# Spreading FP4 scales by TensorE, and a reordered last head in three cross-attention layers

## The chip, the cores and the metric

The kernel runs on one core of a Trainium2 chip, in one launch. The metric is the device time of that launch in microseconds (us). The engines are PE (TensorE), DVE (VectorE), ACT (ScalarE), POOL (GpSimd) and SP (SyncE, which here only issues DMAs).

## The reference, cut to what matters

The program is a stack of twelve layers on `x` (2 batches, 128 tokens, 256 features). The change touches three 16-head cross-attention layers (L0, L2, L3) and the four-bit feed-forward layer (L1_ffn).

```python
# L0_xattn, L2_xattn, L3_xattn: 16 heads of 128, context of 2048 tokens
scores = einsum('bhtd,bhsd->bhts', q, k) / scale      # masked
attn = softmax(scores)                                # P
out = einsum('bhts,bhsd->bhtd', attn, v) @ Wo
x = x + out
...
# L1_ffn: gate, up and down weights are 4-bit codes times scales
W = fp4_value(code) * scale                           # one scale per 32 inputs (two codes a byte)
h = gelu_tanh(x @ Wgate.T) * (x @ Wup.T)              # 256 -> 2048
x = x + h @ Wdown.T
```

For the four-bit layer the scales of gate and up are 8 rows of 2048 numbers each: row `a` holds the scales for the 16 partitions 16a to 16a+15 of a weight tile (8 rows for 128 partitions). Down has 8 rows of 2048 too, so a scale table has 8 x 6144 numbers.

## The kernel before, in words

Each layer is one block; all engines leave a block together (PE, ACT, DVE, POOL and SP meet at its end), and the block of a layer also issues, on SP, the loads of the next layer's weights into the other of two arenas. A block starts with a layer norm on DVE and ACT, and PE turns the result (`xn` to `xnT`).

**Four-bit layer, `fp4_layer` (line 1392).** The codes (3 MB) and the scales are loaded during the block before. The scales are written to all 128 partitions by eight broadcasting DMAs of 16 partitions each (line 214), 384 KB each, 3 MB together, behind the codes in the same queue. The weights are made in eight parts: parts 0 to 3 are quarters of gate and up (512 columns of codes each), parts 4 and 5 the second halves of gate and up (1024), parts 6 and 7 halves of down (1024). For each part DVE masks the bytes (`bytes_of`, line 1476), ACT multiplies by 4097 (`spread`, line 1457), and DVE shifts and masks twice, ORs (`weights`, lines 1492 to 1494) and then multiplies by the scales in two passes (line 1500), which ends with `w_ready` counted up. Before part 0's product with the scales DVE waits for all loads of the arena, `wait_weights` (the last statement before line 1500). PE waits for `w_ready` 2 before the first four column groups `q` of gate and up (line 1436), for 4 before the next four, and for 6 before the last eight; then it multiplies with down (line 1444). DVE forms `inter` from ACT's gelu and PE's up product (line 1508) in `products`: it stands between the parts, as `weights` 0 to 4, products 0 to 3, `weights(5)`, products 4 to 7, `weights(6)`, and so on. All of this is DVE program order.

**16-head layers, `xattn_layer` (line 291).** A unit is one head of one batch, 32 units in all: unit 8i+u is head u//2 of group i, batch u%2. ACT and DVE form P of a unit as two float16 parts, high (ACT line 599) and low (DVE line 729), each in two halves. SP turns both by DMA transpose (lines 377 and 384), and PE multiplies them with the context values: `mix_high` (line 474, 32 matmuls) and `mix_low` (line 484, 16 matmuls), into bank `O[h]`. Per head, ACT copies `O` to `oT` (line 603), PE multiplies by the value weights (`tail_values`, 518), ACT copies (`values_copy`, 609) and PE adds the head's output into bank `OUT` (`tail_out`, 523). The last unit is not turned by DMA: PE turns it (`turn_last`, line 496, part 0 high and part 1 low, 16 transposes each), ACT and DVE copy it back (633, 791) and `mix_last` (509) multiplies it. `scores` fills PE up to three units ahead, so that in the last three units PE has no scores to do. In L2 and L3 POOL also prepares experts' weights for a later layer (lines 2994 to 3011), in the same block.

## Time and profile before

| | us |
|---|---|
| median of 3 runs (lowest, highest) | 1417.43 (1414.89, 1417.97) |
| the profiled execution, its own time | 1408.27 |
| its span, first to last instruction | 1406.5 |
| PE, DVE, ACT, POOL busy | 1231.5, 1088.9, 916.2, 304.7 |

The table reads as follows: the profiled execution lies below the three timed runs, so durations taken from it are set against its own time. The span is what the trace covers; 1.8 us lie around it. Busy PE time includes work that only keeps the engine active (`keep_busy`, line 180).

### The profile page before, as it was taken

Reading aid. Unit: us, or ns where it says so; the run is one execution under the profiler, and the core shown is the slowest. Engines: PE = TensorE matmul, PEld = TensorE weight load, DVE = VectorE, ACT = ScalarE, POOL = GpSimd, SP = SyncE. Lnnn points to the kernel's source line nnn. Section 1 sums busy time; section 2 is a strip of 40 time slices with the busy share of each in tenths; the row PEclk is TensorE's granted clock in tenths of the full one; section 3 lists DMA queues with packets and bytes.
Section 4 is the critical chain, followed back from the end, with each engine's and each line's share of the span. In section 5 each row is a group of like instructions: output and inputs, shape, how many; then the busy total and the mean of one; then the engine's idle time right before and its main releaser. Section 6 shows DMA issues by size and latency. Waiting matters only on the chain. (4 is left out here: it accounts for less than half of the span.)

```text
span 1406.5 us, 25870 instructions
## 1 busy us (share of the span) xinstructions
PE 1231.5 (88%) x10035; PEld 846.6 (60%) x10035; DVE 1088.9 (77%) x2028; ACT 916.2 (65%) x1283; POOL 304.7 (22%) x235
## 2 busy tenths in 40 slices
PE   7999998478879888876989999978898899999987
PEld 3677776353335555555756766765685567666654
DVE  6877885686888999837488898955796798899564
ACT  5877775635667877732267777745695767677664
POOL 3000000001241110000006164250362063452400
PEclk9999999889999999988999999999999999999999
DMA  7999997001008999984169998950662889889700
GB/s 281 178 189 184 179 180 137 18 27 71 1 13 155 193 197 192 200 170 118 55 115 196 175 198 172 174 144 0 208 201 90 149 165 176 171 168 169 141 8 8
DMA packets 548587, 195.77 MB, mean 139 GB/s; under 512 B 534913, under 2 KB 535297, under 8 KB 546945
## 3 DMA queue, kind: packets, MB, share of 16 engines
q1 hardware_dynamic: 548480, 194.35, 69.0%
q8 instruction: 67, 1.10, 0.3%
q14 instruction: 40, 0.32, 0.1%
HBM read 59.83 MB, written 0.26 MB: 43 GB/s over the span
## 5 line engine op out<-in xcount | busy, mean ns | idle before, releaser
L729 DVE SCALAR_TENSOR_TENSOR arena<-L_xattn_sm,L_xattn_rr,arena 128x1024 f16<-128x1024 f32 x192 | 279.0, 1494 | 9.4 <-ACT arena L599 9.4
L460 PE MATMUL ps<-ctxT,L_xattn_qk 128*128 128x512 f16 x1152 | 265.5, 380 | 0.8 <-DVE L_xattn_mx L711 0.5
L584 ACT ACTIVATE L_xattn_sm<-L_xattn_sm,L_xattn_mx 128x2048 f32<-128x2048 f32 x96 | 192.2, 2002 | 78.9 <-DVE L_xattn_mx L711 78.1
L599 ACT ACTIVATE arena<-L_xattn_sm,L_xattn_rr 128x1024 f16<-128x1024 f32 x192 | 210.1, 1141 | 5.2
L474 PE MATMUL ps<-arena,ctx 128*128 128x128 f16 x2976 | 186.0, 222 | 18.4 <-DMA arena<-arena 18.3
L474 PEld LDWEIGHTS ps<-arena,ctx 128*128 128x128 f16 x2976 | 174.5, 99 | 33.1 <-DMA arena<-arena 22.6
L460 PEld LDWEIGHTS ps<-ctxT,L_xattn_qk 128*128 128x128 f16 x1152 | 111.1, 98 | 126.3 <-issue 3.2
L711 DVE CUSTOM_DVE_ANT_0 L_xattn_sm<-ps,L_xattn_bias 128x1024 f32<-128x1024 f32 x96 | 117.2, 1221 | 65.7 <-issue 65.4
L711 DVE CUSTOM_DVE_ANT_0 L_xattn_sm<-ps,L_xattn_bias,L_xattn_mx 128x1024 f32<-128x1024 f32 x96 | 123.2, 1284 | 1.0 <-issue 0.4
L484 PEld LDWEIGHTS ps<-arena,ctx 128*128 128x128 f16 x1488 | 90.8, 98 | 17.1
L484 PE MATMUL ps<-arena,ctx 128*128 128x128 f16 x1488 | 98.3, 219 | 0.0
L180 PE MATMUL ps<-ctxT,identh 128*128 128x512 f16 x328 | 86.9, 401 | 7.6 <-PEq L361 3.0
L2277 PE MATMUL ps<-arena 128*128 128x512 f16 x384 | 92.1, 391 | 0.0
L2289 PE MATMUL ps<-L_xattn_pt,arena 128*32 128x128 f16 x1024 | 70.4, 226 | 22.8 <-DMA L_xattn_pt<-L_xattn_pp 22.4
L2289 PEld LDWEIGHTS ps<-L_xattn_pt,arena 128*32 128x32 f16 x1024 | 59.9, 100 | 41.7 <-DMA L_xattn_pt<-L_xattn_pp 32.2
L589 ACT ACTIVATE L_xattn_rr<-L_xattn_raw,L_xattn_anyone 128x1 f32<-128x1 f32 x96 | 28.2, 293 | 85.8 <-DVE L_xattn_raw L721 84.9
L2419 ACT ACTIVATE L_xattn_pp<-L_xattn_sm,L_xattn_rr 128x1024 f16<-128x1024 f32 x64 | 70.0, 1140 | 20.8 <-DVE L_xattn_rr L2610 20.8
L2619 DVE SCALAR_TENSOR_TENSOR L_xattn_pp<-L_xattn_sm,L_xattn_rr,L_xattn_pp 128x1024 f16<-128x1024 f32 x64 | 79.6, 1285 | 2.7 <-ACT L_xattn_pp L2419 2.4
L2592 DVE CUSTOM_DVE_ANT_0 L_xattn_sm<-ps,arena 128x1024 f32<-128x1024 f32 x64 | 76.5, 1222 | 4.0 <-issue 3.7
L2407 ACT ACTIVATE L_xattn_sm<-L_xattn_sm,L_xattn_nm 128x2048 f32<-128x2048 f32 x32 | 64.1, 2002 | 19.1 <-DVE L_xattn_nm L2601 19.1
L2994 POOL TENSOR_TENSOR L_xattn_inv<-bits,L_xattn_exp 128x48 int32<-128x48 int32 x8 | 2.1, 264 | 304.9 <-DVE L_xattn_exp L2964 304.9
L2277 PEld LDWEIGHTS ps<-arena 128*128 128x128 f16 x384 | 36.2, 100 | 43.8 <-issue 5.1
(541 smaller groups left out, 2107.0 us busy)
## 6 DMA issues: line engine op xcount, KB each, us to landing
L_ffn_ring<-in_L_ffn_experts SPq DMA_DIRECT2D x34, 384.0 KB, 3.8
arena<-in_L_xattn_w SPq DMA_DIRECT2D x36, 320.0 KB, 4.0
arena<-in_L_ffn_experts SPq DMA_DIRECT2D x8, 768.0 KB, 8.7
arena<-in_L_xattn_w SPq DMA_DIRECT2D x6, 640.0 KB, 10.3
arena<-arena SPq DMA_TRANSPOSE x193, 4.5
arena<-in_L_ffn_codes SPq DMA_DIRECT2D x1, 3072.0 KB, 11.4
arena<-in_L_ffn_scales SPq DMA_DIRECT2D x8, 384.0 KB, 22.9
arena<-in_L_attn_w SPq DMA_DIRECT2D x1, 2163.0 KB, 19.2
```

Source lines behind the costliest of these rows:

```text
L180: k.nc.tensor.matmul(k.ps[:, bank, :], k.identh[:], k.ctxT[:, 0, 0, 0:512] if data is None else data, start=True, stop=True)
L460: last = nc.tensor.matmul(ps[:, at, :], qk[:, h // 2, qp, h % 2, b * P:(b + 1) * P], k.ctxT[:, cp, b, at * 512:(at + 1) * 512], start=(a = ...
L474: last = nc.tensor.matmul(O[h][:, b * P:(b + 1) * P], k.ctx[:, cp, b * KT + kt, :], pt[:, b, 0, kt, :], start=(kt == 0 and cp == 0), stop= ...
L484: last = nc.tensor.matmul(O[h][:, b * P:(b + 1) * P], k.ctx[:, 0, b * KT + kt, :], pt[:, b, 1, kt, :], start=False, stop=(kt == KT - 1), s ...
L584: nc.scalar.activation(sm[:, u % 2, :], sm[:, u % 2, :], ACT.Exp, bias=mx[:, u % 2, 1:2], scale=-1.0, accum_out=rs[:, u % 2:u % 2 + 1]).th ...
L599: nc.scalar.mul(pp[:, u % 2, 0, at], sm[:, u % 2, at], rr[:, u % 2:u % 2 + 1]).then_inc(s.p_high, 1)
L711: nc.vector.tensor_tensor_reduce(sm[:, u % 2, half * 1024:(half + 1) * 1024], ps[:, 2 * half:2 * half + 2, :].rearrange("p a n -> p (a n)" ...
L729: nc.vector.scalar_tensor_tensor(pp[:, u % 2, 1, at], sm[:, u % 2, at], rr[:, u % 2:u % 2 + 1], pp[:, u % 2, 0, at], ALU.mult, ALU.subtrac ...
L2277: last = nc.tensor.matmul(ps[:, at, :], qm[:, h % 4, qp, b * P:(b + 1) * P], knT[:, kp, h // 8, b, at * 512:(at + 1) * 512], start=(a == 0 ...
L2289: last = nc.tensor.matmul(O[h // 4][j:j + 32, b * P:(b + 1) * P], v[:, b * KT + kt, h, :, :].rearrange("p s d -> p (s d)"), pt[:, b, part, ...
L2592: nc.vector.tensor_tensor_reduce(sm[:, u % 2, half * 1024:(half + 1) * 1024], ps[:, 2 * half:2 * half + 2, :].rearrange("p a n -> p (a n)" ...
L2619: nc.vector.scalar_tensor_tensor(pp[:, u % 2, 1, at], sm[:, u % 2, at], rr[:, u % 2:u % 2 + 1], pp[:, u % 2, 0, at], ALU.mult, ALU.subtract)\
```

## The change

It does two things.

1. **Four-bit layer.** The scale table is laid out anew, so that the scales of parts 0 to 3 are its first 2048 columns. These are loaded once, as 8 rows (64 KB, semaphore `scale_rows`), and the eight broadcasting DMAs carry only the other 4096 columns. POOL builds an 8x128 selection matrix `sel`, and PE multiplies it with those rows: four float32 matmuls of 512 columns, into PSUM banks 3, 4, 7 and 0. DVE reads the scales of parts 0 to 3 from there. `bytes_of` of parts 4 to 7 moves behind `weights(1)`, and `wait_weights` now stands before part 4's product. `keep_busy` goes from 14 to 16 matmuls and stands behind the four.

2. **16-head layers.** In the last iteration, `turn_last(0)` moves ahead of `mix_high` of unit 30, `turn_last(1)` ahead of its `mix_low`, and `mix_last(0)` ahead of `tail_out` of head 14. Batch 1 of the last head accumulates in bank `PREP` in place of its half of `O[1]`, so the last head's two batches leave one by one (`values_last`, `out_last`, on ACT `mixed_last`, `values_copy_last`).

```diff
-            for a in range(8):
-                sp.dma_start(dst[16 * a:16 * a + 16, :], src[a].partition_broadcast(16)).then_inc(sem, 16)
+            sp.dma_start(dst[0:8, 0:MLP], src[:, 0:MLP]).then_inc(k.g.scale_rows, 16)
+            for a in range(8):
+                sp.dma_start(dst[16 * a:16 * a + 16, MLP:], src[a, MLP:].partition_broadcast(16)).then_inc(sem, 16)
...
+                nc.gpsimd.affine_select(out=sel[:], in_=k.ones[0:8, :], ...).then_inc(s.sel_part, 1)
+                pool.wait_ge(s.sel_part, 1)
+                nc.gpsimd.affine_select(out=sel[:], in_=sel[:], ...).then_inc(s.sel_ready, 1)
...
-                keep_busy(k, 7, 14)
-                pe.wait_ge(g.xnT_ready, k.xt + 1)
+                pe.wait_ge(g.scale_rows, 16)
+                pe.wait_ge(s.sel_ready, 1)
+                for i in range(4):
+                    if i == 3:
+                        pe.wait_ge(g.xnT_ready, k.xt + 1)
+                    nc.tensor.matmul(ps[:, SPREAD[i], :], sel[:], scales[0:8, scale_at[i]:scale_at[i] + FIRST],
+                                     start=True, stop=True).then_inc(s.sc_ready, 1)
+                keep_busy(k, 1, 16)
...
-                for i in range(2, len(parts)):
-                    bytes_of(i)
+                bytes_of(2)
+                bytes_of(3)
...
-                    if i == 0:
+                    if i < 4:
+                        dve.wait_ge(s.sc_ready, i + 1)
+                        scale = ps[:, SPREAD[i], :]
+                    else:
                         wait_weights(k, dve, slot, loaded)
...
-                for i in range(5):
+                weights(0)
+                weights(1)
+                for i in range(4, len(parts)):
+                    bytes_of(i)
+                for i in range(2, 5):
                     weights(i)
```

```diff
+                def values_last(b):
+                    pe.wait_ge(s.oT_ready, XH + b)
+                    at = slice(b * P, (b + 1) * P)
+                    nc.tensor.matmul(TAIL[1 - b][:, at], wv[1], oT[:, at], start=True, stop=True).then_inc(s.oh_psum, 1)
+                def out_last(b):
+                    pe.wait_ge(s.oh_ready, XH + b)
+                    nc.tensor.matmul(OUT[:, b * D:(b + 1) * D], oh[:, b * P:(b + 1) * P], wo[1][:, 1, :], start=False,
+                                     stop=True, skip_group_check=True).then_inc(s.out_done, 1)
...
                         if final and u == UNITS - 1:
+                            mix_last(0)
                             tail_out(*mixed)
                             break
+                        if final and u == UNITS - 2:
+                            turn_last(0)
                         mix_high(i, u, first)
...
                         if final and u == UNITS - 2:
-                            turn_last(0)
+                            turn_last(1)
                         mix_low(i, u)
...
-                turn_last(1)
-                mix_last(0)
-                mix_last(1)
-                tail_values(LASTI, BODY - 1, False)
-                tail_out(LASTI, BODY - 1)
+                values_last(0)
+                mix_last(1)
+                out_last(0)
+                values_last(1)
+                out_last(1)
```

PE at the end of a 16-head layer, before, from `mix_low` of unit 29 on (L474 and L484 are `mix_high` and `mix_low`, L496 `turn_last`, L509 `mix_last`):

```order
L484 MATMUL ps<-arena,ctx 128x128 x16
L474 MATMUL ps<-arena,ctx 128x128 x32
L518 MATMUL ps<-L_xattn_oT,arena 128x256
L496 MATMUL ps<-identh,arena 128x128 x16
L484 MATMUL ps<-arena,ctx 128x128 x16
L523 MATMUL ps<-arena,L_xattn_oh 128x256 x2
L496 MATMUL ps<-identh,arena 128x128 x16
L509 MATMUL ps<-arena,ctx 128x128 x48
L518 MATMUL ps<-L_xattn_oT,arena 128x256
L523 MATMUL ps<-arena,L_xattn_oh 128x256 x2
```

The same stretch of PE in the changed kernel (L531 is `values_last`, L535 `out_last`):

```order
L484 MATMUL ps<-arena,ctx 128x128 x16
L496 MATMUL ps<-identh,arena 128x128 x16
L474 MATMUL ps<-arena,ctx 128x128 x32
L518 MATMUL ps<-L_xattn_oT,arena 128x256
L496 MATMUL ps<-identh,arena 128x128 x16
L484 MATMUL ps<-arena,ctx 128x128 x16
L509 MATMUL ps<-arena,ctx 128x128 x32
L523 MATMUL ps<-arena,L_xattn_oh 128x256 x2
L531 MATMUL ps<-L_xattn_oT,arena 128x128
L509 MATMUL ps<-arena,ctx 128x128 x16
L535 MATMUL ps<-arena,L_xattn_oh 128x256
L531 MATMUL ps<-L_xattn_oT,arena 128x128
L535 MATMUL ps<-arena,L_xattn_oh 128x256
```

Both groups of transposes have moved ahead of a group of unit 30, 32 of the 48 matmuls of L509 have moved ahead of a pair of L523, and the closing pair of steps is cut into two batches.

DVE in the four-bit layer, before, from the layer norm's last row on (L1476 is `bytes_of`):

```order
L139 TENSOR_SCALAR xn<-x,mv,rstd 128x256 x2
L1476 TENSOR_SCALAR arena<-arena 128x512 x2
L1476 TENSOR_SCALAR arena<-arena 128x1024 x4
L1492 TENSOR_SCALAR L_ffn_m<-arena 128x512
L1493 TENSOR_SCALAR arena<-arena 128x512
L1494 TENSOR_TENSOR L_ffn_m<-L_ffn_m,arena 128x512
L1500 TENSOR_TENSOR L_ffn_wgu<-L_ffn_m,arena 128x512 x2
```

The same stretch of DVE in the changed kernel (L1522 is `bytes_of`, L1550 the product with the scales):

```order
L139 TENSOR_SCALAR xn<-x,mv,rstd 128x256 x2
L1522 TENSOR_SCALAR arena<-arena 128x512 x2
L1538 TENSOR_SCALAR L_ffn_m<-arena 128x512
L1539 TENSOR_SCALAR arena<-arena 128x512
L1540 TENSOR_TENSOR L_ffn_m<-L_ffn_m,arena 128x512
L1550 TENSOR_TENSOR L_ffn_wgu<-L_ffn_m,ps 128x512 x2
L1538 TENSOR_SCALAR L_ffn_m<-arena 128x512
L1539 TENSOR_SCALAR arena<-arena 128x512
L1540 TENSOR_TENSOR L_ffn_m<-L_ffn_m,arena 128x512
L1550 TENSOR_TENSOR L_ffn_wgu<-L_ffn_m,ps 128x512 x2
L1522 TENSOR_SCALAR arena<-arena 128x1024 x4
```

The four long `bytes_of` have moved behind two parts, and the product of the first parts reads `ps` in place of `arena`.

PE at the start of the four-bit layer in the changed kernel, between the turning of `xn` and the first column group; before, the row of L1470 was not there and that of L180 had 14 matmuls:

```order
L190 MATMUL ps<-ident,xn 128x128 x4
L1470 MATMUL ps<-arena,L_ffn_sel 128x512 x4
L180 MATMUL ps<-ctxT,identh 128x512 x16
L1482 MATMUL ps<-xnT,L_ffn_wgu 128x256 x64
```

The four spreading matmuls stand ahead of the work that only keeps PE active.

## Rows read from the trace of the kernel before

**Rows 1.** The waits: engine, tile and line, releaser: us, times, longest.

```profile
DVE L_ffn_wgu L1500 <- DMA arena<-in_L_ffn_scales: 7.6, 1, 7.6
DVE x L794 <- PE ps L523: 15.6, 3, 5.2
```

**Rows 2.** Timeline of the four-bit layer: start, us, engine, line [idle before <-releaser].

```profile
629.80 3.17 DVE L1476 TENSOR_SCALAR arena<-arena 128x512 int32<-128x512 int32 x6
...
630.87 5.76 PE L180 MATMUL ps<-ctxT,identh 128*128 128x512 f16 x14
...
632.88 0.42 DVE L1492 TENSOR_SCALAR L_ffn_m<-arena 128x512 int32<-128x512 int32 x1
...
641.93 1.30 DVE L1500 TENSOR_TENSOR L_ffn_wgu<-L_ffn_m,arena 128x512 f32<-128x512 f16 x2 [7.57 <-DMA arena<-in_L_ffn_scales]
...
646.11 0.43 DVE L1492 TENSOR_SCALAR L_ffn_m<-arena 128x512 int32<-128x512 int32 x1
...
646.23 15.78 PE L1436 MATMUL ps<-xnT,L_ffn_wgu 128*128 128x256 f32 x64 [9.59 <-DVE L_ffn_wgu L1500]
...
663.13 14.09 PE L1436 MATMUL ps<-xnT,L_ffn_wgu 128*128 128x256 f32 x64 [1.12 <-DVE L_ffn_wgu L1500]
...
691.07 0.76 DVE L1523 SCALAR_TENSOR_TENSOR x<-ps,x 128x256 f32<-128x256 f32 x2 [12.88 <-PE ps L1444]
```

**Rows 3.** Busy time by windows: PE, PEld, DVE, ACT, POOL, then granted clock, DMA.

```profile
636.00:638.00 2.00, 0.63 (x3) 0.13 (x1) 0.00 (x0) 1.81 (x2) 0.00 (x0) 0.98 1.13 156
```

**Rows 4.** Lines 1476, 1375 and 3386: durations ns min/median/max, starts, forms.

```profile
L1476 DVE TENSOR_SCALAR arena<-arena x8: 421/559/691, 626.7 to 632.3; 128x512 int32<-128x512 int32 x4, 128x1024 int32<-128x1024 int32 x4
L1375 DVE TENSOR_TENSOR x<-ps,x x1: 692/692/692, 625.5 to 625.5; 128x512 f32<-128x512 f32 x1
L3386 POOL TENSOR_SCALAR_AFFINE_SELECT upper<-ones x1: 293/293/293, 3.5 to 3.5; 128x128 f32<-128x128 f32 x1
```

**Rows 5.** The eight scale loads, issued from 607.5 to 610.8: issue to landing.

```profile
DMA to landing us min/median/max: 14.2/22.9/31.0
```

**Rows 6.** Timeline of the end of L0_xattn.

```profile
225.22 2.19 ACT L599 ACTIVATE arena<-L_xattn_sm,L_xattn_rr 128x1024 f16<-128x1024 f32 x2
...
228.09 1.96 PE L474 MATMUL ps<-arena,ctx 128*128 128x128 f16 x32 [2.22 <-DMA arena<-arena]
...
233.08 1.06 PE L496 MATMUL ps<-identh,arena 128*128 128x128 f16 x16
...
233.97 2.84 PE L509 MATMUL ps<-arena,ctx 128*128 128x128 f16 x48
...
237.29 0.70 PE L518 MATMUL ps<-L_xattn_oT,arena 128*128 128x256 f32 x2 [0.47 <-ACT L_xattn_oT L603]
...
238.45 1.13 PE L523 MATMUL ps<-arena,L_xattn_oh 128*128 128x256 f32 x4 [0.46 <-ACT L_xattn_oh L609]
...
239.62 0.69 DVE L794 TENSOR_TENSOR x<-ps,x 128x512 f32<-128x512 f32 x1 [5.20 <-PE ps L523]
...
240.82 1.28 ACT L147 ACT_TABLE_LOAD   x1 [2.42 <-PEq L361]
```

**Rows 7.** Timeline of the end of L2_xattn.

```profile
920.27 2.19 ACT L599 ACTIVATE arena<-L_xattn_sm,L_xattn_rr 128x1024 f16<-128x1024 f32 x2
...
921.08 1.96 PE L474 MATMUL ps<-arena,ctx 128*128 128x128 f16 x32 [1.17 <-DMA arena<-arena]
...
930.90 2.92 POOL L3011 TENSOR_TENSOR arena<-arena,L_xattn_exp 128x768 bf16<-128x768 f32 x2
...
932.63 0.69 DVE L794 TENSOR_TENSOR x<-ps,x 128x512 f32<-128x512 f32 x1 [5.20 <-PE ps L523]
...
934.25 1.28 ACT L147 ACT_TABLE_LOAD   x1 [2.84 <-PEq L361]
```

**Rows 8.** Timeline of the end of L3_xattn.

```profile
1313.98 2.91 POOL L3011 TENSOR_TENSOR arena<-arena,L_xattn_exp 128x768 bf16<-128x768 f32 x2
...
1316.21 0.69 DVE L794 TENSOR_TENSOR x<-ps,x 128x512 f32<-128x512 f32 x1 [5.20 <-PE ps L523]
```

More of the change, by code:

```diff
@@ L508, in mix_last @@
                             for cp in range(2 - part):
-                                last = nc.tensor.matmul(O[1][:, P:2 * P], k.ctx[:, cp, KT + kt, :], pt[:, 1, part, kt, :],
+                                last = nc.tensor.matmul(PREP[:, P:2 * P], k.ctx[:, cp, KT + kt, :], pt[:, 1, part, kt, :],
                                                         start=(kt == 0 and cp == 0 and part == 0),
@@ L626, in body @@
                             q_copy(*group)
+                        if final and u == UNITS - 2:
+                            last_copy(0, 0)
+                            last_copy(0, 1)
                         if head:
                             values_copy(*head, first and u == 2)
-                def last_copy(part, half):
-                    act.wait_ge(s.last_psum, 2 * part + half + 1)
-                    act.wait_ge((s.mixed_hi, s.mixed_lo)[part], XH * B - 2)
-                    nc.scalar.copy(pt[:, 1, part, half * KT // 2:(half + 1) * KT // 2, :], TURNED[2 * part + half])\
-                        .then_inc((s.last_hi, s.last_lo1)[part], 1)
-                if opening:
-                    act.wait_ge(g.keys_loaded1, 16)
-                    nc.scalar.copy(k.ctxT[:, 0, 1, :], raw_context(k, 1)[0]).then_inc(g.keys_high1, 1)
                 q_copy(0, 0)
@@ L656, in _ @@
                 iterations(act, body)
[L657 to L658 removed]
                 last_copy(1, 1)
[L660 to L661 removed]
+                mixed_last(0)
+                values_copy_last(0)
+                mixed_last(1)
+                values_copy_last(1)
             @block.gpsimd
@@ L1409, in fp4_layer @@
         gelu = sb("gelu", [P, RING, T])
+        sel = sb("sel", [8, P])
         inter = k.arena[slot][:, 3 * MLP:5 * MLP].rearrange("p (q t) -> p q t", q=NG)
@@ L1419, in _ @@
                 stage_loads(sp)
+            @block.gpsimd
+            def _(pool):
+                nc.gpsimd.affine_select(out=sel[:], in_=k.ones[0:8, :], compare_op=ALU.is_ge, fill=0.0, base=0,
+                                        pattern=[[1, P]], channel_multiplier=-16).then_inc(s.sel_part, 1)
+                pool.wait_ge(s.sel_part, 1)
+                nc.gpsimd.affine_select(out=sel[:], in_=sel[:], compare_op=ALU.is_ge, fill=0.0, base=15,
+                                        pattern=[[-1, P]], channel_multiplier=16).then_inc(s.sel_ready, 1)
             @block.tensor
@@ L1495, in weights @@
                     vals = mm.bitcast(F16).rearrange("p (n a) -> p n a", a=2)
-                    if i == 0:
+                    if i < 4:
+                        dve.wait_ge(s.sc_ready, i + 1)
+                        scale = ps[:, SPREAD[i], :]
+                    else:
                         wait_weights(k, dve, slot, loaded)
+                        scale = scales[:, scale_at[i]:scale_at[i] + width]
                     to = at % MLP
@@ L1500, in weights @@
                         last = nc.vector.tensor_tensor(dests[at // MLP][:, par, to:to + width], vals[:, :, par],
-                                                       scales[:, at:at + width], ALU.mult)
+                                                       scale, ALU.mult)
                     last.then_inc(s.w_ready, 1)
@@ L3487, in lay_out @@
                                         rows(L("L1_ffn_down_W_packed").T)], axis=1)
-    d["L1_ffn_scales"] = np.concatenate([L("L1_ffn_gate_scales").T, L("L1_ffn_up_scales").T,
+    halves = [L(f"L1_ffn_{w}_scales").T[:, h * MLP // 2:(h + 1) * MLP // 2] for h in range(2) for w in ("gate", "up")]
+    d["L1_ffn_scales"] = np.concatenate([*halves,
                                          L("L1_ffn_down_scales").T.reshape(8, 8, D).transpose(1, 0, 2).reshape(8, -1)],
```

29 lines of the change are left out of this document (22 added, 7 removed).

## The prediction

> **What bounds the kernel now.** I read the waits first, then the timelines of the two places that the change touches. No single engine bounds the whole program: each layer has its own chain, and a layer's start follows from the end of the one before. So what matters is which wait ends last inside the two kinds of block.
>
> In the four-bit layer one wait stands out: DVE stands still for 7.6 us before its first product with the scales, and the releaser is the load of the scales [rows 1]. The reader is to see in the timeline that it is a true stop: DVE has part 0 unpacked at 641.93 - 7.57 = 634.36, and PE, behind it, starts its first column group only at 646.23, after 9.6 us idle [rows 2]. The last of the eight scale loads was issued at 610.8 and they take up to 31.0 us to land, which ends at 641.8 [rows 5]; that is the release. After it DVE is busy without a gap until 663.1, and PE, which has done its first eight column groups by 662.0 (646.23 + 15.78), waits 1.12 us for DVE's parts 4 and 5 [rows 2]. From 663.13 on PE runs through gate, up and down to DVE's last step at 691.07, 27.9 us later [rows 2]. So the layer's end hangs on when DVE finishes part 5, and that on when it may begin to multiply by the scales.
>
> At the end of the 16-head layers the last wait is DVE's for the last `tail_out`: 15.6 us in three layers, 5.2 each [rows 1]. In L0 it sets the block's end: DVE ends at 240.31 and the next block's first row on ACT is at 240.82, 0.51 later [rows 6]. In L2 it does not: DVE ends at 933.32, but the next block's row comes at 934.25, 0.93 later; POOL's last row ends at 933.82, 0.43 ahead of it [rows 7]. In L3 both end together, POOL at 1316.89 and DVE at 1316.90 [rows 8].
>
> **Four-bit layer.** DVE first. Before, six `bytes_of` stand between the layer norm and part 0, from 629.80 to 632.88 [rows 2]. A short one is 0.42 us and a long one 0.69 [rows 4]; overlapped they fill 3.08 us, some 0.7 for the two short and 2.4 for the four long. Only the short ones stay ahead, so part 0's unpacking starts at 630.5. It takes 634.36 - 632.88 = 1.48 and is done at 632.0.
>
> Then DVE waits for the first spreading matmul. PE could start it where it now starts `keep_busy`, at 630.87 [rows 2]. Its rows are loaded ahead of all broadcasts; the first broadcast, six times as large, took 14.2 us from 607.5 [rows 5], so the rows are there by 622. `sel` takes POOL two operations of 0.29 each [rows 4] at the block's start, while PE is idle until 630, so by 628. A float32 matmul of 256 columns is two records, 14.09 / 64 = 0.22 us apart at the high clock [rows 2], so one of 512 columns is 0.88, and 1.76 at the low one. The clock is low at 631: fourteen float16 matmuls of 512 columns take 5.76 us, 0.41 each, which is 1.2 GHz [rows 2], and it is high (0.98 granted, 2.4 GHz) only between 636 and 638, after PE had been active since about 630 [rows 3]. So the first spread ends at 630.87 + 1.7 plus 0.2 to drain, 632.8, and DVE loses 0.85 us to it. If the spreads were free of this, that 0.85 would be gained too (upper bound); the later ones, at 634.5, 636.2 and 637.1, are ahead of DVE.
>
> DVE needs 646.11 - 641.93 = 4.18 us from the first product to the end of part 1's [rows 2]: 632.85 + 4.18 = 637.03. The four long `bytes_of` now stand here, in the way: 2.4, so 639.45. From part 2's first row to the release of part 5 it was 663.13 - 646.11 = 17.02; that gives 656.45, against 663.13: 6.7 us earlier. Behind the moved `bytes_of` ACT's multiplications of parts 4 to 7 come later, but part 4 is wanted only 5.7 us later.
>
> The product now reads its scales from PSUM. A DVE operation with 512 columns and one operand in PSUM took 0.69 [rows 4], two from SBUF take 1.30 [rows 2], 0.65 each; eight of them cost at most 0.3, and I take 0.1. **Sum for this layer: 6.6 us.**
>
> The Trainium skill speaks against this step here: "VectorE: DVE Perf Modes", section "The TRN2 errata — SBUF-src ops pay a fixed extra latency per instruction", gives a Vector operation with a PSUM source 120 fixed cycles and one with SBUF sources 58. By it the eight products would cost 0.5 us more, the layer would gain 6.2, and the time would be 1409.7; the rows above bear out less.
>
> PE must not become the bound. After the spreads (637.1) come sixteen `keep_busy` of 0.22 at the high clock, until 640.6; eight column groups take 14.1 (64 records, as in the second half [rows 2]), until 654.7, 1.8 us ahead of DVE. The remaining scales, two thirds of the bytes, are wanted by part 4's product at about 647.7, while all landed at 641.8 before [rows 5]. So these edits lie under DVE's work; the two extra `keep_busy` and SP's ninth DMA too. If the clock rose only with the column groups, PE would be 2.3 us late (a rival below).
>
> **L0.** `turn_last(0)` is put into PE's wait for the DMA transpose: PE idles 2.22 us up to 228.09. It waits for the last P-high, whose second half is ready at 225.22 + 2.19 = 227.41. Sixteen transposes take 233.97 - 233.08 = 0.89, the second eight 0.45: done at 227.9, so `mix_high` of unit 30, which is queued behind, still starts at 228.09 [rows 6]. What follows holds 0.89 us less and one half-width value matmul more (some 0.25): the last mixing ends at 236.81 - 0.64 = 236.17. ACT's copies of the turned P-high come at 228 to 230, before it is wanted elsewhere. From that end to DVE's add it was 239.62 - 236.81 = 2.81, two PE steps of 0.70 and 1.13 and two copies of ACT among it [rows 6]. With one batch left, PE's steps shrink by about 0.25 and 0.48 and the copies by 0.1 each (a half-width operation keeps its fixed part), and `out_last(0)` stands in the way by 0.1: 1.97. DVE would start at 238.14, **1.5 us earlier**. Bounds: 0.6 if the halves cost as much as wholes, 2.0 if everything halves.
>
> **L2 and L3.** Here the wait that is filled is shorter, 1.17 us in L2: `mix_high` starts at 921.08, but P-high is complete only at 920.27 + 2.19 = 922.46. With the second eight transposes `mix_high` starts at 922.95, 1.87 later [rows 7]. Less 0.89, plus 0.25, less 0.84 at the tail: DVE ends 0.4 us later, at 933.7. With 0.51 behind it that is 934.2, just what POOL sets now (934.25): nothing lost, nothing gained. That cover gone, it would cost 0.4. In L3 POOL ends with DVE, so at most 0.1 can be had [rows 8], and at worst L2's 0.4 is lost. I take zero for both.
>
> **Sum:** 6.6 + 1.5 + 0 + 0 = 8.1 us. The profiled execution's own time is 1408.27 (span 1406.5), so it would be 1400.2. The median of the runs is 9.2 higher, and there the same difference gives **1409.3**.
>
> **Rivals.**
> *All three 16-head layers gain 1.5.* For it: the same 5.2 us wait in each [rows 1]. Against: POOL's ends [rows 7, 8] and the late P-high. It takes 3.0 more: 1406.3.
> *PE bounds the four-bit layer.* If the spreads and `keep_busy` all run at the low clock, they end at 630.9 + 4 x 1.71 + 16 x 0.43 = 644.6, the column groups at 658.7 instead of 656.4: 2.3 us of the gain go, 1411.6. For it: the clock was low for 6 us after PE began [rows 2, 3]; against: PE now stays active without a break.
> *The four-bit layer gives back nearly all*, because something in part 4's way (its scales, ACT's multiplications) takes the place of the wait: only L0's 1.5 stays, 1415.9. Against: 5.9 us between the old landing and the new need.
> *Slower: the scale rows land late.* PE's spreads, and all of PE behind them, wait for one small DMA. If its eight long rows landed only with the end of the queue, at 641.8, the first product would follow at 643.7, PE (idle meanwhile, clock low) would do the other spreads by 648.8 and the sixteen matmuls by about 653.5, and eight column groups by 667.6. That is 4.5 later than 663.1; with L0's 1.5, 1420.4. It decides from a landing at about 637 on that nothing is gained in this layer. Against: it is issued first, and a larger load behind it took 14.2 us [rows 5].
>
> **How the numbers follow.** Chances: forecast 0.62, all three layers 0.13, PE bound 0.16, gain given back 0.06, late rows 0.03. A measurement of this kernel can tell about 0.2%, 2.8 us, from no change. The first three are faster by more: 0.91; given back is within it: 0.06; late rows: 0.03 slower. The forecast's own bounds (0.85 up in the four-bit layer and 0.5 in L0; 0.9 in L0, 0.2 for PSUM and 0.8 in L2 and L3 down) span 1407.9 to 1411.2. With the two neighbouring cases, 1406.3 and 1411.6, and the scatter of 3 us among the runs before, the range is 1405.4 to 1413.2.
>
> **What would show it.** Right: DVE's first product with the scales near 633 to 634, waiting for PE under 1 us; PE's first column group near 640.5; DVE still the releaser before the ninth group, some 6.5 us earlier counted from the block's start; in L0 the add 1.5 us earlier from the last P-high; in L2 the same distance to the next block, with a gap before L474. Wrong: a DVE wait for PE of several us, L1436's successor starting at the low clock, or POOL ending well before the blocks of L2 and L3.

## The result, and the profile after

| us | before | after |
|---|---|---|
| median (lowest to highest, runs) | 1417.43 (1414.89 to 1419.47, 5) | 1406.71 (1402.35 to 1409.59, 5) |
| profiled execution, its own time | 1408.27 | 1406.71 |
| its span | 1406.5 | 1405.0 |
| mean granted TensorE clock in it | 0.964 | 0.962 |

The ratio on record is 0.9912, with a 95% interval of 0.9895 to 0.9929: 12.5 us less, 10.0 to 14.9. The forecast was 8.1 less. The direction was right. The size was too small: 0.9912 of 1417.43 is 1405.0, just under the range's lower end of 1405.4. The five runs of each kernel in the table give a smaller difference than that ratio: 10.7 us between the medians, and 10.7 between the means (1417.3 and 1406.6). By them the changed kernel's 1406.71 lies inside the range, near its lower end; the record does not show what makes the two figures differ. And the two profiled executions are only 1.5 us apart, so what the profiles show and what the runs show has to be told apart. One run of the experiments below, the sixth of f2, took 2109.57 us at a mean granted clock of 0.553 and is left out of every figure.

The four-bit layer in the timeline of the changed kernel (start, us, engine, line, and in brackets the idle time before it and its releaser). They answer to [rows 2]:

```profile
629.20 1.28 ACT L147 ACT_TABLE_LOAD   x1 [3.34 <-PEq L1301]
629.56 0.36 POOL L1458 TENSOR_SCALAR_AFFINE_SELECT L_ffn_sel<-L_ffn_sel 8x128 f32<-8x128 f32 x1
632.71 1.13 PE L190 MATMUL ps<-ident,xn 128*128 128x128 f32 x4 [4.80 <-DVE xn L139]
633.24 0.42 DVE L1538 TENSOR_SCALAR L_ffn_m<-arena 128x512 int32<-128x512 int32 x1
633.77 7.19 PE L1470 MATMUL ps<-arena,L_ffn_sel 8*128 8x512 f32 x8
635.95 1.28 DVE L1550 TENSOR_TENSOR L_ffn_wgu<-L_ffn_m,ps 128x512 f32<-128x512 f16 x2 [1.23 <-PE ps L1470]
640.89 5.53 PE L180 MATMUL ps<-ctxT,identh 128*128 128x512 f16 x16
646.26 15.92 PE L1482 MATMUL ps<-xnT,L_ffn_wgu 128*128 128x256 f32 x73
657.09 2.36 DVE L1550 TENSOR_TENSOR L_ffn_wgu<-L_ffn_m,arena 128x1024 f32<-128x1024 f16 x2
```

The reader is to see that the stop of 7.57 us is gone: DVE waits 1.23 us for the first spread and is busy from there on. PE's column groups have no idle time in their row. Its sixteen groups begin at 646.26 and the product with down at 673.88, so the first eight end half way, at about 660.1, while DVE released part 5 at 657.09 + 2.36 = 659.45. So PE, not DVE, is now last, by 0.6 us.

The same stretch by windows (PE, PEld, DVE, ACT, POOL busy; then granted clock, DMA share, GB/s):

```profile
633.77:640.90 7.13, 7.13 (x10) 2.50 (x9) 5.73 (x11) 1.70 (x4) 0.00 (x0) 0.50 0.91 247
640.90:644.30 3.40, 3.40 (x10) 1.19 (x10) 3.33 (x7) 3.40 (x4) 0.00 (x0) 0.50 1.03 423
644.30:646.20 1.90, 1.90 (x9) 0.92 (x8) 1.83 (x5) 1.72 (x2) 0.00 (x0) 0.87 0.40 162
646.30:660.30 14.00, 14.00 (x67) 12.72 (x66) 13.72 (x20) 3.34 (x8) 0.00 (x0) 1.00 0.00 0
```

PE was busy for 7.1 us without a break in the first window, and the granted clock stayed at 0.50 (1.2 GHz). It rose at about 644.8 (0.87 over the third window), 3.9 us after the full-row filling matmuls had begun. In the kernel before it rose at about 636.1 (0.98 over the window of [rows 3]), 5.2 us after its filling matmuls had begun [rows 2].

The waits, which answer to [rows 1] (us, times, longest):

```profile
DVE x L821 <- PE ps L535: 19.1, 3, 6.4
DVE L_ffn_wgu L1550 <- PE ps L1470: 1.2, 1, 1.2
```

DVE's wait for the last `tail_out` is longer, 6.4 us for 5.2, though L0's end comes sooner: DVE now stops earlier (its copy of P-low ends sooner), and waits more. The sum of a wait says little about the path.

The ends of L0, L2 and L3, for [rows 6 to 8]:

```profile
229.00 2.19 ACT L612 ACTIVATE arena<-L_xattn_sm,L_xattn_rr 128x1024 f16<-128x1024 f32 x2
230.20 0.62 PE L496 MATMUL ps<-identh,arena 128*128 128x128 f16 x8 [0.56 <-ACT arena L612]
231.24 0.62 PE L496 MATMUL ps<-identh,arena 128*128 128x128 f16 x8 [0.42 <-ACT arena L612]
231.74 1.96 PE L474 MATMUL ps<-arena,ctx 128*128 128x128 f16 x32
...
241.75 0.69 DVE L821 TENSOR_TENSOR x<-ps,x 128x512 f32<-128x512 f32 x1 [6.38 <-PE ps L535]
242.94 1.28 ACT L147 ACT_TABLE_LOAD   x1 [1.98 <-PEq L361]
...
919.74 2.19 ACT L612 ACTIVATE arena<-L_xattn_sm,L_xattn_rr 128x1024 f16<-128x1024 f32 x2
920.94 0.62 PE L496 MATMUL ps<-identh,arena 128*128 128x128 f16 x8 [1.87 <-ACT arena L612]
...
932.43 0.69 DVE L821 TENSOR_TENSOR x<-ps,x 128x512 f32<-128x512 f32 x1 [6.38 <-PE ps L535]
933.62 1.28 ACT L147 ACT_TABLE_LOAD   x1 [1.98 <-PEq L361]
...
1301.59 2.19 ACT L612 ACTIVATE arena<-L_xattn_sm,L_xattn_rr 128x1024 f16<-128x1024 f32 x2
...
1312.22 2.92 POOL L3065 TENSOR_TENSOR arena<-arena,L_xattn_exp 128x768 bf16<-128x768 f32 x2
...
1314.28 0.69 DVE L821 TENSOR_TENSOR x<-ps,x 128x512 f32<-128x512 f32 x1 [6.38 <-PE ps L535]
1315.91 1.28 ACT L174 ACT_TABLE_LOAD   x1 [2.41 <-PEq L361]
```

From the last P-high to the next block's first row: L0 13.94 us where it was 15.60; L2 13.88 for 13.98; L3 14.32 for 14.05. In L0 the add came 12.75 us after the last P-high for 14.40. Of these 1.65 us 0.13 lie ahead of `mix_high` of unit 30 and 1.52 behind its start, where the edit takes work out. In L2 PE now idles 1.87 us before the first eight transposes, waiting for ACT's P-high. In L3 the add came 0.17 us sooner (12.69 for 12.86), but the next block 0.27 later; POOL's last row, not DVE's, ended last there, at 1315.14.

**Where the time went, by layers of the two profiles** (from a layer's first row of the layer norm on DVE, `bn_stats`, to the next layer's):

```
            before   after              before   after
L0_xattn    237.39  239.49   L2_xattn   241.92  244.48
L0_attn      71.68   71.69   L2_attn     52.94   51.94
L0_ffn       26.73   26.71   L2_ffn      85.86   85.59
L1_xattn    267.73  268.17   L3_xattn   244.36  244.76
L1_attn      20.38   20.59   L3_attn     33.42   33.41
L1_ffn       65.00   59.04   L3_ffn      55.64   55.65
```

The four-bit layer is 5.96 us shorter by this count. But its layer norm now begins 0.93 us after the block's start where it was 0.72, and L1_attn, which is counted up to there, grew by those 0.21 (its two short `bytes_of` take 0.97 us for 0.76; what slows them is not shown). From block start to block start it is 5.75 us. So the places that the change touches sum to 5.75 + 1.66 + 0.10 - 0.27 = **7.24 us**. Yet L0_xattn and L2_xattn are longer as wholes, at units that the change doesn't touch. L2's unit 26 shows how. These are the same instructions on PE, before and after:

```profile
879.15 1.13 PE L447 MATMUL ps<-L_xattn_qT,arena 128*128 128x512 f32 x2 [2.19 <-ACT L_xattn_qT L574]
880.11 1.95 PE L474 MATMUL ps<-arena,ctx 128*128 128x128 f16 x32
```

```profile
876.27 1.51 PE L447 MATMUL ps<-L_xattn_qT,arena 128*128 128x512 f32 x2 [2.18 <-ACT L_xattn_qT L587]
877.57 3.25 PE L474 MATMUL ps<-arena,ctx 128*128 128x128 f16 x32
```

```profile
876.30:879.70 3.40, 3.40 (x22) 2.49 (x23) 3.40 (x2) 2.67 (x4) 3.32 (x3) 0.59 0.98 181
883.10:886.50 3.40, 3.40 (x48) 2.81 (x47) 3.27 (x7) 0.68 (x1) 0.00 (x0) 1.00 1.06 196
```

The last two rows are windows of the changed kernel: after PE had idled 2.18 us the granted clock was 0.59 on average for 3.4 us, and the unit took 9.44 us in place of 7.79. In the profile before the same idle time of 2.19 was followed by the high clock. In L0_xattn unit 0 is 1.1 us longer and unit 3 is 3.1 longer (8.13 for 5.00), and both lie over low stretches twice as long as before or not there before; with unit 13's 0.9, for which I found no such stretch, and less the 1.2 by which units 2 and 5 are shorter, they make up for the 1.7 gained at the layer's end and more. In L2_xattn another 0.7 lies ahead of unit 30 (6.09 for 5.38 between its exponential and the one before). With plain copies in place of the DMA transposes that interval is 5.32 or 5.33 in each kernel of the first series below, so it hangs on the transposes; whether the change has a part in it is open.

### The profile page after: what moved, and what is told of

The parts are those of the page before. It is cut to its first block and busy times, and to the rows that moved or that the text cites. A ratio compares the mean times of both kernels' runs of the same rounds, so it can differ in the third digit from the quotient of the medians.

```text
span 1405.0 us, 25920 instructions
## 1 busy us (share of the span) xinstructions
PE 1237.8 (88%) x10051; PEld 848.8 (60%) x10051; DVE 1088.2 (77%) x2028; ACT 916.3 (65%) x1289; POOL 305.4 (22%) x237
## 5 line engine op out<-in xcount | busy, mean ns | idle before, releaser
L474 PE MATMUL ps<-arena,ctx 128*128 128x128 f16 x2976 | 188.8, 223 | 11.9 <-DMA arena<-arena 11.7
L474 PEld LDWEIGHTS ps<-arena,ctx 128*128 128x128 f16 x2976 | 177.4, 100 | 26.9 <-DMA arena<-arena 15.6
L484 PEld LDWEIGHTS ps<-arena,ctx 128*128 128x128 f16 x1488 | 90.8, 98 | 17.1
L484 PE MATMUL ps<-arena,ctx 128*128 128x128 f16 x1488 | 98.3, 219 | 0.0
L180 PE MATMUL ps<-ctxT,identh 128*128 128x512 f16 x330 | 86.3, 397 | 7.6 <-PEq L361 3.0
L180 PEld LDWEIGHTS ps<-ctxT,identh 128*128 128x128 f16 x330 | 31.6, 101 | 49.6 <-issue 24.3
```

The costliest lines, as they stand in the source:

```text
L180: k.nc.tensor.matmul(k.ps[:, bank, :], k.identh[:], k.ctxT[:, 0, 0, 0:512] if data is None else data, start=True, stop=True)
L474: last = nc.tensor.matmul(O[h][:, b * P:(b + 1) * P], k.ctx[:, cp, b * KT + kt, :], pt[:, b, 0, kt, :], start=(kt == 0 and cp == 0), stop= ...
L484: last = nc.tensor.matmul(O[h][:, b * P:(b + 1) * P], k.ctx[:, 0, b * KT + kt, :], pt[:, b, 1, kt, :], start=False, stop=(kt == KT - 1), s ...
```

## The experiments

The changed kernel was not run again, nor was either edit alone with the DMA transposes in it; only the kernel before was timed again, 40 times beside the experiments. So whether something in the change, with the transposes, brings more than its places show is a rival that stays untested. All kernels that follow hold plain DMA copies of the same bytes in their place, so that P and the last layer's weights are not turned, and their times stand against each other only.

```diff
-sp.dma_start_transpose(pt[:, u % 2, 0, :, :], pp[:, u % 2, 0, :])
+sp.dma_start(pt[:, u % 2, 0, :, :].rearrange("p t q -> p (t q)"), pp[:, u % 2, 0, :])
```

The plain copies land in 2.9 us (median) where the transposes take 4.5. "Tail" below is the time from the last exponential of a 16-head layer to the next block's first row.

### First series: each edit alone

f1 is the kernel before, f2 the changed one, f3 has the four-bit edit alone, f4 that of the 16-head layers alone.

> The kernel before with its 193 + 64 + 8 DMA transposes (P in the cross-attention layers, weights in the last layer) made plain DMA copies of the same bytes, so that P and those weights are not turned: the base for the next three. The time itself may be anything near 1417 us: a copy keeps the order of the work, but its issue and landing may take less than the 2 us and 4.5 us of a transpose. No theory is tested by it alone; its profile shows how much of the 16-head layers' length hangs on the DMA.

> The changed kernel with plain copies. Theory A (each part is worth what its place in the trace shows: four-bit layer 6.0, L0 1.6, L2 0.1, L3 -0.3): 7.4 us under f1. Theory B (part of the gain lies elsewhere, in the cross-attention layers away from the edited places): 10 to 13 us under f1.

> Only the four-bit layer's part of the change, with plain copies. Theory A: 6.0 us under f1. Theory B, if the four-bit part carries the excess: 9 us or more; if not, 6.

> Only the 16-head part, with plain copies. Theory A: 1 to 2 us under f1, nearly all in L0. Theory B: 4 to 7 us under f1, with layers that are shorter ahead of their last three units.

```
                 median us (runs)   L1_ffn   tails L0 / L2 / L3
f1 before        1404.20 (6)        65.00    16.36 / 17.38 / 17.27
f2 both          1405.39 (5)        59.33    16.70 / 18.85 / 19.34
f3 four-bit      1402.24 (4)        59.33    16.37 / 17.27 / 17.38
f4 16-head       1408.68 (6)        64.07    16.70 / 19.33 / 18.90
```

The four-bit edit shortens its layer by 5.7 us (f1 to f3; 5.5 from block start to block start), about as with the real transposes, but the median by 2.0 only. No theory of f2, f3 or f4 came true by the medians: f3 was to be 6 us or more under f1 and is 2.0, f2 was to be 7 us or more under f1 and is 1.2 over it, f4 was to be under f1 and is 4.5 over it. The edit of the 16-head layers *costs* here: 0.34 + 1.95 + 1.63 = 3.9 us at the three tails (f4 less f1), and 4.5 by the medians; f2 less f3 gives 3.9 at the tails and 3.2 by the medians. The reason stands in f2's timeline of L2's end, beside f1's:

```profile
909.41 0.62 PE L496 MATMUL ps<-identh,arena 128*128 128x128 f16 x8 [1.88 <-ACT arena L612]
910.45 1.03 PE L496 MATMUL ps<-identh,arena 128*128 128x128 f16 x8 [0.42 <-ACT arena L612]
911.27 3.15 PE L474 MATMUL ps<-arena,ctx 128*128 128x128 f16 x32
```

```profile
912.19 1.96 PE L474 MATMUL ps<-arena,ctx 128*128 128x128 f16 x32
```

With the turning moved ahead, PE idles 1.88 us for ACT's P-high; then the clock is low (0.61 over 3.4 us) and the 32 matmuls of `mix_high` take 3.15 us for 1.96. With copies that land sooner the wait that was to be filled isn't there, and the moved work makes one. The changed kernel has the same idle times in L2 and L3 (1.87 and 1.40), but in its profiled execution no low stretch fell on them.

### Second series: a pause before each copy

So that PE waits for P as it does for the transposes, SP loads 2 KB and waits for it before each of the 16-head layers' copies.

```diff
+sp.dma_start(little[:], k.ident[:, 0:4]).then_inc(s.pause, 16)
+sp.wait_ge(s.pause, 16 * n)
 sp.dma_start(pt[...].rearrange("p t q -> p (t q)"), pp[...])
```

g1 is the kernel before, g2 both edits, g3 only the moved turning and mixing (no split by batch), g4 only the split (`values_last`, `out_last`, own bank) with the old order. g3 and g4 have the old four-bit layer.

> The kernel before with plain copies in place of the DMA transposes (so P and the last layer's weights are not turned), and in the three 16-head layers a pause ahead of each copy: SP loads 2 KB and waits for it, so that a copy lands some 4.5 to 5 us after its turn begins, as a transpose did. Base for the next three. If the pause does its work, PE's wait before the matmuls of unit 30 in L0 is about 2 us again, and the distance from the last unit's exponential to the next block is 17 to 18.5 us in the three layers.

> The changed kernel with the same stand-in. Read at its places. Theory A (the work moved ahead fills a wait that exists only where the transposed P comes late): from the last exponential to the next block 1.6 us shorter in L0, 0 in L2 and L3, the four-bit layer 6 shorter. Theory C (PE now idles longer in one piece ahead of unit 30, and the clock falls more often in the last stretch): 1.5 us longer in one or both of L2 and L3, with the granted clock at 0.5 in a part of it, as with plain copies.

> Same stand-in; of the 16-head edit only the order (both groups of turning matmuls and the mixing of P-high moved ahead), the last head's two batches still leave together; nothing of the four-bit edit. Theory A: L0 0.7 to 0.9 us shorter than g1, L2 and L3 0.5 to 1.2 us longer where POOL does not hide it. If the order were worth the whole 1.6 in L0, the split would be worth nothing.

> Same stand-in; of the 16-head edit only the split of the last head by batch, with its own bank; order as before; nothing of the four-bit edit. Theory A: 0.8 us shorter than g1 in L0, and in L2 and L3 too unless POOL ends the block (then 0 to 0.4). If the split is worthless: 0 in L0.

```
                 median us (4 runs)     tails L0 / L2 / L3
g1 before        1460.82                22.47 / 19.72 / 20.20
g2 both          1448.58                18.04 / 19.33 / 17.72
g3 order only    1451.48                18.52 / 19.96 / 19.19
g4 split only    1460.48                20.17 / 20.12 / 17.63
```

Here PE does wait, and the whole gains: 12.2 us by the medians (g1 to g2). In the two profiled executions 4.43 + 0.39 + 2.48 = 7.3 stand at the tails and 64.5 - 59.4 = 5.1 in the four-bit layer, 12.4 together; but these two are 19.3 us apart as wholes, so that 12.2 and 12.4 agree is in part luck. Nor are the 7.3 the edit's worth in the changed kernel. The stand-in overshoots: g1's tails are 19.7 to 22.5 us where 17 to 18.5 were expected, its wait ahead of unit 30 in L0 is 3.46 us for about 2, and each of its tails holds a stretch of low clock, g2's only that of L2. The start of `mix_high` of unit 30 in L0, in g1 and in g2:

```profile
247.39 2.71 PE L482 MATMUL ps<-arena,ctx 128*128 128x128 f16 x32 [3.46 <-DMA arena<-arena]
```

```profile
246.62 1.96 PE L482 MATMUL ps<-arena,ctx 128*128 128x128 f16 x32 [0.88 <-DMA arena<-arena]
```

From there to the end of the last `tail_out` it is 13.1 us in g1 and 10.3 in g2, where the kernels with the real transposes have 11.5 and 10.0. So of L0's 4.43 some 1.5 is what the edit gives there, some 1.4 is g1's low stretch, and the rest lies ahead of `mix_high`. Theory A had 1.6 for L0 and nothing for L2 and L3, and its numbers fell in all but L2.

The parts don't come apart so well. By the medians the order alone gives 9.3 and the split alone 0.3; by the tails 4.7 and 4.5. Runs of one kernel lie up to 19 us apart in this series (g2: 1441.4 to 1460.0), so the medians can't tell the one from the other. What the split does is plain in PE's rows of the end of L0, in g4 and g1:

```profile
252.99 1.95 PE L517 MATMUL ps<-arena,ctx 128*128 128x128 f16 x32
254.78 0.44 PE L539 MATMUL ps<-L_xattn_oT,arena 128*128 128x128 f32 x2
...
257.32 0.70 PE L543 MATMUL ps<-arena,L_xattn_oh 128*128 128x256 f32 x2 [0.36 <-ACT L_xattn_oh L649]
```

```profile
254.91 2.84 PE L517 MATMUL ps<-arena,ctx 128*128 128x128 f16 x48
...
259.39 1.13 PE L531 MATMUL ps<-arena,L_xattn_oh 128*128 128x256 f32 x4 [0.46 <-ACT L_xattn_oh L617]
```

From the first of these mixings to the end of the last `tail_out` it is 257.32 + 0.70 - 252.99 = 5.03 us with the split and 5.61 without: 0.6 us. The order takes the sixteen transposes of P-high, 0.9 us [rows 6], out of this tail. The two together are the 1.5 of the forecast, and the 1.52 found behind the start of `mix_high` in the changed kernel.

### Third series: what brings the clock up, and a warm start

h1 is f1 with filling matmuls of 8 rows; h2 is f3 with fourteen more full-row ones in PE's wait at the block's start; h3 and h4 are f3 and f1 again.

```diff
 h1:
-keep_busy(k, 7, 14)
+for _ in range(14):
+    nc.tensor.matmul(ps[:, 7, :], k.identh[0:8, :], k.ctxT[0:8, 0, 0, 0:512], start=True, stop=True)
 h2:
+keep_busy(k, 1, 14)
 xT_tensor(k, pe, k.xn, 0, n, cols=True)
```

> Kernel before with plain copies; the fourteen filling matmuls at the start of the four-bit layer read 8 of their 128 rows (their output is read by nobody). Theory A (matmuls of 8 rows do not bring TensorE's clock up, whatever their data type and whatever they keep the engine busy for): the granted clock stays at 0.5 through the fourteen, each takes the 0.43 us of the low clock, 6.0 us in all, and it is still 0.5 when the first group's matmuls begin 9.6 us later. Rival B (in the change it was the float32 data, or merely that the fall came later, and rows have no part): the fourteen run the last of their row at 0.22 us as they do with 128 rows, and the clock rises during them, 6.8 us after its fall, as in the kernel before.

> Changed four-bit layer alone with plain copies, and fourteen filling matmuls of 128 rows more in TensorE's wait at the layer's start, ahead of the turning of the normed rows (TensorE is idle there for 3.5 us). Theory A: the clock does not fall before the spreads, so they take 3.6 us in place of 7.2; DVE's products of parts 0 to 3 wait less (the first 0.4 to 0.9 us less) and TensorE reaches its first group before DVE has part 1, so that the eighth group ends with DVE's fifth part and not 0.9 us after: the layer becomes 0.9 to 1.7 us shorter than the 59.3 us of the run without it, unless the clock falls during the spreads; then (rival B, 8-row matmuls count as idleness) it falls some 3 us into them, and the gain is 0.9 at most. Rival C: the fillers delay the turning (they last till after the normed rows are there): the layer is the same or up to 1 us longer.

> The changed four-bit layer alone with plain copies, the kernel of the second series again, beside the run above on one chip. If the places of TensorE's low clock fall by chance from one execution to the next, its layer stays at 59.3 us to 0.1, while the sum of the other eleven layers of its profile differs from that of the first time (1343.0) by steps of about 1.6 us, up to some 5 us. If they are fixed by the program, the other eleven are the same to 0.3 us.

> The kernel before with plain copies again, on the same chip as the run above. Its four-bit layer 65.0 us. The difference of the medians to the run above is the four-bit change's worth with plain copies a second time: 5.7 us by the layers of the profiles, and 2.0 by the medians of the second series. Theory A (chance of the low clock's places, with medians of five carrying an error of about 1.5 us each): between 3 and 8 now. Rival B (something in the program takes back 3 to 4 us of the layer's gain each time): 1 to 3 again.

In h1 the clock stayed low through all fourteen, float16 as they are, and on into the column groups. Windows of h1:

```profile
623.20:629.40 6.20, 6.17 (x15) 1.88 (x14) 3.35 (x7) 6.05 (x8) 0.00 (x0) 0.50 1.02 127
639.50:645.00 5.50, 5.46 (x13) 4.41 (x14) 5.33 (x10) 0.47 (x1) 0.00 (x0) 0.50 0.51 208
```

So it is not float32 that kept the clock down in the changed kernel, and not the time for which PE was busy: in the kernel before the clock rose behind the same count of matmuls over 128 rows [rows 2, 3]. The four-bit layer of h1 took 66.1 us; with 128 rows it took 65.0, 64.3 and 66.8 in f1, h4 and i1, so that length tells nothing.

h2's PE in the four-bit layer:

```profile
620.66 3.18 PE L180 MATMUL ps<-ctxT,identh 128*128 128x512 f16 x14 [1.33 <-PEq L1274]
624.13 0.74 PE L190 MATMUL ps<-ident,xn 128*128 128x128 f32 x4 [0.29 <-DVE xn L139]
624.81 3.70 PE L1444 MATMUL ps<-arena,L_ffn_sel 8*128 8x512 f32 x8
628.44 5.31 PE L180 MATMUL ps<-ctxT,identh 128*128 128x512 f16 x16
633.59 14.09 PE L1456 MATMUL ps<-xnT,L_ffn_wgu 128*128 128x256 f32 x64
649.74 15.78 PE L1456 MATMUL ps<-xnT,L_ffn_wgu 128*128 128x256 f32 x64 [2.06 <-DVE L_ffn_wgu L1524]
```

```profile
624.81:628.50 3.69, 3.69 (x10) 1.47 (x10) 3.55 (x8) 1.63 (x3) 0.00 (x0) 1.00 0.88 224
629.50:632.80 3.30, 3.30 (x9) 1.18 (x8) 3.27 (x7) 1.73 (x2) 0.00 (x0) 0.50 1.02 414
650.00:653.30 3.30, 3.30 (x9) 2.56 (x9) 3.27 (x7) 0.00 (x0) 0.00 (x0) 0.50 0.00 0
```

At the high clock (first window) the spreads take 3.70 us in place of 7.19, DVE's wait for the first is gone, and PE is ahead of DVE by 2.06 us before the ninth group, much as the prediction had it (1.8). But about 1 us behind the spreads the clock drops for 3.4 us (second window), and PE's idle 2.06 us is followed by another low stretch (third window), so the last eight groups take 15.78 us for 14.0. The layer is 59.09 us against 59.31: of the 0.9 to 1.7 expected, 0.2. The medians, 1395.81 against 1398.48, differ by less than the runs of either.

h3 and h4 repeat f3 and f1: layers of 59.31 and 64.32 us, medians 1398.48 and 1399.18, 0.7 apart, which is less than either theory of h4 had. Outside the four-bit layer h3's profile is 3.6 us shorter than f3's (1339.4 and 1343.0), the sum of single layers that differ by up to 3.8 us in both directions: L1_xattn took 267.1 and 263.8 us, L3_xattn 242.6 and 246.4, in the same kernel.

### Fourth series: does a layer's length hang on when it starts?

In f1 and h4 L2_xattn took 238.8 and 237.4 us with the old four-bit layer, in f3 and h3 244.0 with the new one (but h1, with the old one, had 244.1, and h2, with the new one, 240.7). That suggested that the edit shifts the later layers against the clock's low stretches, the same way each time. i1 and i3 are f1 and f3 a third time; i2 and i4 have a delay on DVE ahead of the four-bit layer's last add.

```diff
 dve.wait_ge(s.out_psum, 1)
+chain(nc.vector.tensor_tensor(m[:], m[:], m[:], ALU.bitwise_or))              # i2: 1.25 us
+chain(nc.vector.tensor_scalar(m[:, 0:1024], m[:, 0:1024], 0xFF, None, ALU.bitwise_and))  # i4
+chain(nc.vector.tensor_scalar(m[:, 0:512], m[:, 0:512], 0xFF, None, ALU.bitwise_and))    # i4
```

> The kernel before with plain copies, a third time, as the measure for the two kernels with an added pause. Its four-bit layer 64.3 to 65.0 us, its L2_xattn 237.4 to 238.8 us as in both earlier profiles.

> The same, and one operation of 1.25 us more on DVE between the end of the four-bit layer's last product and its add: nothing but 1.3 us of delay for all that follows. Theory A (the other layers' lengths depend on where the stretches of low clock fall against them, and so on how late they start): L2_xattn starts 1.3 us later against the clock's changes, where three kernels of these series had it (the edited four-bit layer's two, and the one with 8-row filling matmuls), and takes 243.9 to 244.1 in place of 238.8 at most; the profile's layers from L2 on are 6.5 us later at L2_attn, and the median of all runs 3 to 7 us above the kernel without the pause. Rival B (layers' lengths have nothing to do with when they start): 1.3 us longer, L2_xattn the same.

> The changed four-bit layer alone, plain copies, a third time. Four-bit layer 59.3 us, L2_xattn 243.9 to 244.0 us as in both earlier profiles; median against the first kernel of this call 0.5 to 3 us less, as twice before, in place of the layer's 5.7.

> The same, and 1.0 us more on DVE at the same place (a row of 1,024 and one of 512 elements). Theory A: L2_xattn then starts where it does in the kernel before, takes 237.4 to 238.8 us, and the kernel with this delay is 3 to 5.5 us faster than the one without; against the first kernel of this call it wins 5 us or more, what the layer itself saved. Rival B: 1.0 us slower than without it.

```
                  median us (runs)   L1_ffn   L2_xattn
i1 before         1402.29 (5)        66.79    242.68
i2 before + 1.25  1403.26 (6)        67.65    239.06
i3 four-bit       1396.13 (6)        59.64    240.27
i4 four-bit +0.96 1394.29 (5)        60.79    242.54
```

Theory A fell. L2_xattn took 242.7 us in the same kernel that had shown 238.8 and 237.4, and 240.3 in the one that had shown 244.0 twice. The delay in i2 cost 1.0 us, about itself; i4 came out 1.8 *faster* than i3 (8.0 under i1), which is inside the scatter of either. So which units meet a low stretch changes from execution to execution of one kernel. The edit's worth in three pairs of medians was 2.0, 0.7 and 6.2; over all 17 and 16 runs the mean spans are 1400.1 and 1397.6, 2.4 us apart, give or take 2.6. The layer's own 5.7 (5.9 on average over the three pairs of profiles, less the 0.2 of its late start) is just outside that. Including the delayed kernels, less their delays, it is 3.7 give or take about 2.2, within which 5.7 lies.

## Why the prediction was off

**Where DVE stands in the four-bit layer: right.** The stop is gone, the products start 6.75 us after the block's start where 6.2 was forecast, DVE waited 1.23 us for the first spread (0.85), because PE came to it 0.34 us later in the block and DVE's product followed its start by 2.18 us for 1.98; DVE itself was ready 0.16 later. "Late scale rows" and "part 4's scales" did not come up: the broadcasting loads landed in 24.1 us at most, against 31.0 before [rows 5], and PE waited for no rows.

**"It is high only between 636 and 638, after PE had been active since about 630", and from that the later spreads at 0.9 us and `keep_busy` at 0.22: this step failed.** It took for granted that the clock would rise behind the spreads, which have 8 rows, as it had behind the filling matmuls of 128 rows. In the changed kernel and in h1 the granted clock stayed at 0.50 through 7.1 and 6.2 us of matmuls of 8 rows. All spreads ran at 1.2 GHz, PE reached its first group 17.1 us after the block's start in place of 13.9, and is 0.6 us *behind* DVE where it was to be 1.8 ahead. The rival "PE bounds the four-bit layer" had the mechanism; its price of 2.3 was too high, because the last filling matmuls did run at the high clock (PE was 1.2 us sooner than the rival had it) and DVE was 0.4 later than forecast. The term was 6.6 and measured 5.75.

**The products from PSUM: right.** Two of them took 1.28 us, against 1.30 from SBUF [rows 2]: nothing, where 0.1 was allowed. The Trainium skill, "VectorE: DVE Perf Modes", section "The TRN2 errata — SBUF-src ops pay a fixed extra latency per instruction", gives the PSUM source the longer fixed part, by which they would have been dearer; the trace doesn't agree.

**L0: right.** 1.66 us for 1.5: 0.9 from the order (the transposes, counted from the rows of before), 0.6 from the split (g4 against g1) and 0.13 ahead of `mix_high`. **L2 and L3: right.** In L2 the add came 12.69 us after the last P-high where it was 12.36, later by the 0.3 that was forecast as 0.4, and POOL's cover hid it; -0.10 and +0.27 for zero and zero. That no low stretch followed PE's new idle times of 1.87 and 1.40 us there is luck of the one execution: with plain copies f2 and f4 had one in both layers. The rival of 1.5 in all three layers is out.

So the sum by places is 7.24 for 8.1.

**"The median of the runs is 9.2 higher, and there the same difference": this step failed, and it is what carried the time out of the range.** It puts everything outside the edited places at nothing. By the ratio on record the difference was 12.5 us, 5.3 more than the places show; between the medians it was 10.7, 3.5 more; between the profiled executions 1.5. The profiled execution of the changed kernel is its median run. That of before, at 1408.27, was an unusual one: in 40 later runs of the same kernel none was under 1411.8, and none had a mean granted clock over 0.961, where that profile shows 0.964. A mean clock c means that 2 x (1 - c) of the span ran at the low level: 101 us in that execution, 126 on average in the 40 runs (0.9556). Among these runs 1 us more of low clock goes with 0.27 us more of time (correlation 0.84; 0.18 to 0.38 in the four groups of them). By that slope an execution with 101 us would take 1409.8 us of span, and this one took 1406.5, so its low clock explains two thirds of how short it was. The five runs of the changed kernel average 0.9604, 111 us. The 15 us less low clock would be worth 4.0 us by that slope, and of the 11.6 us between the mean spans (1416.5 and 1404.9) 7.6 remain, beside the 7.24 found by places. So the account closes, but only so far: the slope is a correlation among runs, the 40 runs are those taken beside the experiments and not the five beside the changed kernel, and it is argued, not shown.

**What stays open** is why the changed kernel's runs had less low clock. Its four-bit layer has about 3 us less of it in the two profiles (a mean of 0.88 over 59.04 us for 0.87 over 65.00), though PE now works through nearly all of it. Five runs with a standard deviation of 2.7 us leave their mean uncertain by about 3, so chance can make most of the missing 3.5 to 5.3 us. With plain copies the medians went the other way (2.4 or 3.7 found where the layer gives 5.7). A fixed shift by when the layers start was tested and fell. An effect of one of the edits that needs the real transposes was not tested.

## What to carry to other kernels

A small matmul put on an idle TensorE is priced at the clock that it will find. Here matmuls of 8 rows ran 7.1 us at the low clock that they found, and the clock came up only behind matmuls of 128 rows. With fourteen of these ahead of them (h2) they took 3.70 us in place of 7.19, but low stretches fell behind them and behind an idle 2.06 us, and the layer gained 0.2 us only: look at the whole stretch, not at the matmuls alone. A stretch of work moved into a wait pays only while the wait is there and its input is ready; here the edit of the 16-head layers cost 3.9 us at the tails where P came early (f4), and won 1.5 us behind the start of `mix_high` where P came late. And before a difference between two profiles is read, set each profiled execution against its kernel's timed runs, by time and by mean granted clock, and then read the difference by places, not by span.

## What the runs showed of the hardware

Matmuls of 8 rows kept PE busy for 7.1 us (float32) and 6.2 us (float16) at a granted clock of 0.50, and one run of the former, begun at the high clock, was followed by a low stretch of 3.4 us though PE never idled. Outside the long waits the clock also fell for 3.4 us after idle times of only 1.9 to 2.2 us, in some executions and not in others, at 1.2 to 1.7 us a time. The 40 runs of the kernel before have a standard deviation of 2.9 us, and 0.27 us of time go with 1 us of low clock in them. POOL's second `affine_select` on 8x128, in place, took 0.36 us, the first 0.28.
